# One core: the column part of each tridiagonalisation step ahead of its inner product, and the first normalisation's statistics on ScalarE

## What is computed

```python
h = maximum(layernorm(x), 0)                       # first normalisation
deg = A.sum(0) + A.sum(1) - diagonal(A);  L = diag(deg) - A
L_norm = d_inv_sqrt * L * d_inv_sqrt
_, U = eigh(L_norm)                                # 128 x 128, written out by hand in the kernel
x = x + U @ (relu((U.T @ h) @ W1 + b1) @ W2 + b2)  # first layer, for each batch
h = maximum(layernorm(x), 0)                       # second normalisation
x = x + second_layer(h)                            # two products with adj, then LSTMs over windows of 1 to 4 nodes
```

## Time and profile before

| | |
|---|---|
| median of 3 runs | 1527.23 us (1527.11 to 1527.44) |
| profiled execution | 1526.4 us, its span 1524.7 us |
| PE busy | 1196.6 us, 78% of the span |
| DVE busy | 1127.3 us, 74% |
| ACT busy | 816.7 us, 54% |
| POOL busy | 507.2 us, 33% |
| granted TensorE clock, mean | 0.938 of full |

### The profile page before, as it was taken

How to read it: one execution, slowest core, us unless ns; L and a number is a source line. 1 busy time by engine, 2 the same in 40 slices (tenths; PEclk the granted TensorE clock), 3 DMA queues, 4 the chain that set the end, 5 groups by cost and what they waited for, 6 DMA issues and landing times.

```text
span 1524.7 us, 26089 instructions
## 1 busy us (share of the span) xinstructions
PE 1196.6 (78%) x7121; PEld 1070.2 (70%) x7121; DVE 1127.3 (74%) x5950; ACT 816.7 (54%) x2699; POOL 507.2 (33%) x1426
## 2 busy tenths in 40 slices
PE   5677777777626500079999999999999999999998
PEld 4556666666515500068889899898998989989897
DVE  8999999999999999977757645555464554645545
ACT  2323222232419800012478687786877868778676
POOL 0288888888888888820000200000000000000000
PEclk9999999999959955569999999999999999999999
DMA  9300000000000000003100000000000000000001
GB/s 268 78 1 1 1 1 1 1 1 1 1 1 1 1 0 1 0 22 90 56 1 1 28 0 14 14 0 28 0 14 14 0 28 0 16 12 0 28 1 29
DMA packets 43624, 28.75 MB, mean 19 GB/s; under 512 B 1520, under 2 KB 39440, under 8 KB 43536
## 3 DMA queue, kind: packets, MB, share of 16 engines
q1 hardware_dynamic: 43536, 27.81, 6.7%
HBM read 19.42 MB, written 8.39 MB: 18 GB/s over the span
## 4 chain that ended last, share of the span: by engine, by line
PE 54%; DVE 40%; ACT 3%; issue 3%; ACTq 0%; DVEq 0%
PE bank L796 13%; PE bank L786 10%; PE bank L791 8%; PE bank L799 7%; DVE PV L1190 5%; DVE RC L1184 4%; PE bank L599 3%; DVE PV L1120 3%; DVE sc L933 2%; PE bank L716 2%; PE bank L768 2%; PE bank L760 2%; PE bank L724 2%; DVE sc L944 2%; PE bank L754 2%
## 5 line engine op out<-in xcount | busy, mean ns | idle before, releaser
L796 PE MATMUL bank<-spare,wT 128*128 128x256 f32 (+2 forms) x1408 | 311.3, 321 | 0.0
L533 ACT ACTIVATE PV<-bank,bias 128x256 f32<-128x256 f32 (+2 forms) x704 | 303.9, 435 | 0.0
L533 ACT ACTIVATE BIG<-bank,bias 128x128 f32<-128x128 f32 (+2 forms) x544 | 227.5, 418 | 121.1 <-PE bank L799 101.9
L796 PEld LDWEIGHTS bank<-spare,wT 128*128 128x128 f32 x1408 | 234.8, 191 | 13.2
L786 PE MATMUL bank<-spare,wT 128*128 128x128 f32 (+2 forms) x1088 | 228.1, 320 | 4.1 <-DVE spare L1427 2.7
L1413 DVE TENSOR_TENSOR BIG<-BIG,PV 128x128 f32<-128x128 f32 (+2 forms) x192 | 62.9, 328 | 206.1 <-ACT BIG L533 206.1
L786 PEld LDWEIGHTS bank<-spare,wT 128*128 128x128 f32 x1088 | 168.7, 190 | 22.4 <-DVE spare L1427 9.1
L799 PE MATMUL bank<-spare,wT 128*128 128x128 f32 (+2 forms) x768 | 169.7, 303 | 0.0
L425 ACT ACTIVATE sc<-bank 128x1 f32<-128x1 f32 x127 | 21.7, 171 | 257.9 <-PE bank L599 257.9
L599 PE MATMUL bank<-ident 128*128 128x2 f32 x254 | 74.4, 362 | 97.5 <-DVE ident L949 96.3
L791 PE MATMUL bank<-spare,wT 128*128 128x128 f32 (+2 forms) x768 | 141.7, 307 | 3.7 <-DVE spare L1425 1.2
(11 more groups left out here) (393 smaller groups left out, 2788.4 us busy)
## 6 DMA issues: line engine op xcount, KB each, us to landing
spare<-in_x SPq DMA_DIRECT2D x32, 256.0 KB, 4.1
out<-X SPq DMA_DIRECT2D x32, 256.0 KB, 2.4
spare<-in_L_gnn_Wih SPq DMA_DIRECT2D x4, 256.0 KB, 5.4
spare<-in_L_gnn_Whh SPq DMA_DIRECT2D x4, 256.0 KB, 5.2
W<-in_L_gnn_W SPq DMA_DIRECT2D x2, 64.0 KB, 3.2
Wg<-in_L_gnn_Wg SPq DMA_DIRECT2D x2, 64.0 KB, 2.5
adj<-in_adj SPq DMA_DIRECT2D x1, 64.0 KB, 1.7
X<-in_x SPq DMA_DIRECT2D x4, 0.5 KB, 17.0
```

The source lines that it names most:

```text
L533: last = nc.scalar.activation(gate_out[q][i][:, 0:T], gate(i, q, T), ACT.Tanh if q == GATE_G else ACT.Sigmoid, bias=bias[:, at:at + 1])
L796: last = nc.tensor.matmul(gate(i, q, T), wT[:, 0, p - 1, q * D:(q + 1) * D], xt, start=True, stop=(j == 0))
```

## The change

DVE's scalar pairs are formed in another way and order. A new pair `MU` is column 0 and 1 of `UC` times `u_t`, formed beside the reciprocal; `HV, HG` is `MU` times `h_k`. The wait for ACT's column comes ahead of `HUM, HU`, that for ACT's row ahead of `HV, HG`. `PT` (the column part) is put ahead of the inner product. `x_statistics` is taken from DVE and becomes three activations on ACT, at the end of ACT's part of a step: a copy that sums, a small one that makes minus the mean, and a square that sums. `STAT_LAG` is 2; `stat_at` puts one batch in each step from step 2 on, and two in steps 10, 20 and 30, so that all 128 are done in step 126. `variance` for the first normalisation shrinks to one operation, and `inverse` to six of the same kind written out.

```diff
-        bn_done = sem("bn_done")
+        stats_done = sem("stats_done")
...
+        MU = 8
...
-        BN_LAG = 16
+        STAT_LAG = 2
+
+        def stat_at(k):
+            return max(0, k - STAT_LAG) + sum(k > 10 * (e + 1) for e in range(BATCH - STEPS + STAT_LAG))
...
+            def x_statistics(b):
+
+                total, lower, at = ln[:, 0, b:b + 1], ln[:, 3, b:b + 1], X[:, b, :]
+                if b % (BATCH // X_CHUNKS) == 0:
+                    act.wait_ge(x_in[b // (BATCH // X_CHUNKS)], 16)
+                nc.scalar.activation(QP[0], at, ACT.Copy, accum_out=total).then_inc(stats_done, 1)
+                act.wait_ge(stats_done, 3 * b + 1)
+                nc.scalar.activation(lower, total, ACT.Copy, scale=-1.0 / D).then_inc(stats_done, 1)
+                act.wait_ge(stats_done, 3 * b + 2)
+                nc.scalar.activation(QP[1], at, ACT.Square, bias=lower,
+                                     accum_out=ln[:, 1, b:b + 1]).then_inc(stats_done, 1)
...
                 nc.scalar.activation(eB[:, k:k + 1], sign(k), ACT.Identity, scale=two_sigma(k)).then_inc(e_ready, 1)
+                for b in range(stat_at(k), stat_at(k + 1)):
+                    x_statistics(b)
...
-                if k >= BN_LAG:
-                    x_statistics(k - BN_LAG)
...
                 n_h = step(V.reciprocal(h_k, S(DEN)))
+                dve.wait_ge(hv, n_ut)
+                n_mu = step(V.tensor_scalar(S(MU, 2), UC[:, k, 0:2], u_t, None, ALU.mult))
                 dve.wait_ge(hv, n_h)
                 dve.wait_ge(u_ready, k + 1)
+                dve.wait_ge(acol_ready, k + 1)
+                n_hu = step(V.tensor_tensor(S(HUM, 2), UC[:, k, 1:3], h_k.to_broadcast([N, 2]), ALU.mult))
+                dve.wait_ge(hv, n_mu)
                 if t + 1 < N:
                     dve.wait_ge(row_ready, k + 1)
-                n_hu = step(V.tensor_tensor(S(HUM, 2), UC[:, k, 1:3], h_k.to_broadcast([N, 2]), ALU.mult))
-                n_hv = step(V.tensor_scalar(S(HV, 2), UC[:, k, 0:2], u_t, h_k, ALU.mult, ALU.mult))
+                step(V.tensor_tensor(S(HV, 2), S(MU, 2), h_k.to_broadcast([N, 2]), ALU.mult))
 
                 dve.wait_ge(pb_ready, k + 1)
-                dve.wait_ge(acol_ready, k + 1)
-                step(V.tensor_tensor_reduce(out=wB[:, live(k)], in0=banks[1][:, live(k)], in1=uk[:, live(k)],
-                                            scale=h_k, scalar=0.0, op0=ALU.mult, op1=ALU.add, accum_out=S(K3)))
                 dve.wait_ge(hv, n_hu)
                 n_pt = step(V.scalar_tensor_tensor(out=S(PT), in0=B[1][:, nxt], scalar=S(HUM), in1=S(ACOL),
                                                    op0=ALU.mult, op1=ALU.subtract))
+                step(V.tensor_tensor_reduce(out=wB[:, live(k)], in0=banks[1][:, live(k)], in1=uk[:, live(k)],
+                                            scale=h_k, scalar=0.0, op0=ALU.mult, op1=ALU.add, accum_out=S(K3)))
...
-            for b in range(STEPS - BN_LAG, BATCH):
-                x_statistics(b)
             hear(rows)
-            go(V.tensor_copy(dB[:], B[3]))
+            n_dB = go(V.tensor_copy(dB[:], B[3]))
             V.tensor_tensor(Q1, B[4], QH, ALU.mult).then_inc(q_in, 1)
-            dve.wait_ge(bn_done, BATCH)
...
-            variance(slice(0, BATCH))
+            dve.wait_ge(stats_done, 3 * BATCH)
+            V.tensor_scalar(ln[:, 1, :], ln[:, 1, :], 1.0 / D, LN_EPS, ALU.mult, ALU.add).then_inc(ln_var, 1)
             n_e = go(V.scalar_tensor_tensor(out=M[0], in0=eB[:], scalar=-1.0, in1=eB[:], op0=ALU.mult, op1=ALU.max))
+            n_E = go(V.tensor_copy(EV[:], eB[:].unsqueeze(1).to_broadcast([N, LEVELS, N])))
+            dve.wait_ge(v_, n_dB)
             n_D = go(V.tensor_copy(D4[:], dB[:].unsqueeze(1).to_broadcast([N, LEVELS, N])))
-            n_E = go(V.tensor_copy(EV[:], eB[:].unsqueeze(1).to_broadcast([N, LEVELS, N])))
...
-            inverse(slice(0, BATCH))
+            off, var, inv, shift = (ln[:, c, :] for c in range(4))
+            op(V.reciprocal(inv, inv))
+            op(V.tensor_tensor(off, inv, inv, ALU.mult))
+            op(V.tensor_tensor(off, off, var, ALU.mult))
+            op(V.tensor_scalar(off, off, -0.5, 1.5, ALU.mult, ALU.add))
+            op(V.tensor_tensor(inv, off, inv, ALU.mult))
+            V.tensor_tensor(shift, shift, inv, ALU.mult).then_inc(ln_done, 1)
```

More of the change, by code:

```diff
@@ L891, in step @@
                 return h.n
[L893 to L897, removed]
             def householder(k, before):
@@ L1377, in statistics @@
                     at = it * (STREAMS * GB) + i * GB + b
-                    V.bn_stats(stats[:, at, :], X[:, at, :]).then_inc(bn_done, 1)
+                    V.bn_stats(stats[:, at, :], X[:, at, :]).then_inc(stats_done, 1)
             for it in range(ROUNDS):
                 if it == ROUNDS - 2:
-                    dve.wait_ge(bn_done, BATCH + FIRST)
+                    dve.wait_ge(stats_done, 3 * BATCH + FIRST)
                     variance(slice(0, FIRST))
@@ L1444, in last_statistics @@
                 elif (n, i) == (CELL + 8, 3):
-                    dve.wait_ge(bn_done, 2 * BATCH)
+                    dve.wait_ge(stats_done, 4 * BATCH)
                     variance(slice(FIRST, BATCH))
```

## The result

| | before | after |
|---|---|---|
| median time | 1527.34 us (1527.11 to 1527.44, 4 runs) | 1516.64 us (1515.92 to 1516.81, 4 runs) |
| profiled execution | 1526.4 us, span 1524.7 | 1516.81 us, span 1515.1 |

The medians are 10.7 us apart, a ratio of 0.9930; the ratio on record is 0.9927, with a 95% interval of 0.9915 to 0.9939. The forecast was 1516.7.

What follows compares the result with a forecast made beforehand. The chain of waits lay on PE (54%) and DVE (40%), with POOL 9.0 us behind. DVE's 16.6 us gain, some 6 lost waiting for POOL, left 10.5: profiled 1526.4 to 1515.9, median 1516.7, range 1512.5 to 1521.

Steps and rivals of the forecast that it cites:

- main mechanism: At the sign before `eig_done`: of DVE's 16.6 us gain, 6 us turn into a wait for POOL; chance 0.74.
- (a): DVE's order inside a Householder step: 0.12 us in some 28 steps, 0.10 in 99, 13.3 us gained.
- (b): `bn_stats` taken out of DVE's step: 1.0 us gained over all, between 0 and 4.4.
- (c): DVE's seam after step 126: statistics and variance operations shrink, 4.1 us gained.
- (d): ACT's three statistics activations take 1.25 us (1.0 to 1.7) and fit the 1.84 us gap before the root.
- double steps: Steps 10, 20 and 30, two batches on ACT: 2.5 us each, over the free gap; -1.8 us in all.
- R4: Rival: Sqrt and Square not in one ACT table, two loads a step, near 1775 us; chance 0.02.
- sum on DVE's path: All DVE terms to the sign, 13.3 + 1.0 + 4.1 - 1.8 = 16.6 us gained, L1341 reached at 651.5.
- POOL's path: POOL's leaf work ends 1.3 us earlier, at 657.8, from its earlier start; 1.5 us allowed either way.
- R1: Rival: order gives under 0.04 us a step, DVE stays last at the sign; 1523.9, up to 1518 us; chance 0.10.
- R2: Rival: POOL's end follows DVE's lighter load, so the whole 16.6 us arrive; 1510.6 us; chance 0.05.
- R3: Rival: ACT's statistics ahead of the root become the bound, slower, 1562 us; chance 0.05.

Runs made afterwards that it cites:

- experiment 1: The kernel after with 15 instead of 16 of POOL's QR sweeps; 1513.66 us.
- experiment 2: The kernel before with 15 instead of 16 of POOL's QR sweeps; 1526.78 us.
- experiment 8: The kernel after without `MU`, 15 QR sweeps, plus an extra PE column product into an unread bank ahead of the real one; 1560.37 us.
- experiment 7: The kernel after without `MU` (`HV, HG` from one two-scalar instruction) and with 15 instead of 16 QR sweeps; 1510.16 us.
- experiment 5: The kernel after without `MU`: `HV, HG` again from one two-scalar instruction, the new order kept; 1517.84 us.
- experiment 4: The kernel after with the old order and no `MU` in the step, so only the statistics move to ACT; 1524.11 us.
- experiment 3: The kernel before with only the new order and `MU` in the step, `bn_stats` left on DVE; 1519.66 us.
- experiment 6: The kernel after with the square of each statistics batch on ACT done three times; 1525.82 us.

## Why the prediction was right, point by point

**The main mechanism held.** The gain on DVE's path exceeded POOL's slack, and the rest became an idle time before the sign, released by POOL's L417 (3.36 us). Experiments 1 and 2 show it from both sides.

**(a) The order: 13.3 forecast, 8.6 measured alone. This is the term that was mis-sized.** The first 16 steps gave 0.12, as forecast (R came 2.89 us after x_c and now comes 2.77), the next 16 gave 0.09. The middle ones gave 0.05 to 0.07 and the narrow ones 0.04 to 0.05, not 0.10. Two things were read wrongly. First, `PT` comes 0.13 behind `HV, HG`, not 0.08, in every part of the loop. Second, the bound "R cannot start before L606's end plus 0.03" took the product as ready too early; it is ready 0.11 us after its modelled end, as experiment 8 shows. In the earlier trace rows that is 254.79 + 0.11 = 254.90, so R at 254.98 had 0.08 us to gain and not 0.16. This second limit decides in the narrow steps: in after, R stands right at it in 23 of the last 32 steps. The bounds, 0 to 20 us, held the measured 8.6.

`MU` is the smaller half of the story. It was costed at 0.06 for `HUM, HU`, and from the reciprocal on it costs 0.07 (0.26 against 0.19). Put against the old two-scalar instruction it loses: without it DVE comes to the sign 2.8 to 2.9 us earlier (experiments 7 and 5). This was not costed as a variant of its own.

**(b) `bn_stats` out of the step: +1.0 forecast**; -1.0 by itself (experiment 4), +0.8 beside the new order (364.68 for after against 365.50 for experiment 3). The same steps agree from profile to profile within some 0.2 us (364.68 and 364.64 in after and experiment 1, 374.06 and 374.13 in before and experiment 2, 361.62 and 361.84 in experiments 5 and 7), so the two signs are repeatable. But they are not shown to be the price of `bn_stats`. Take the median step of each 16 and add up: beside the new order that gives 360.3 us with `bn_stats` (experiment 3) and 360.5 and 360.1 without (after, experiment 1), the same, and the 0.8 lies in single steps that last 0.1 to 0.3 us longer than their neighbours. Beside the old order it gives 369.2 and 369.4 with it (before, experiment 2) and 370.1 without. So in a typical step its removal gains nothing in either order. Why the single long steps fall as they do stays open.

**(c) The seam: 4.1 forecast, 3.87 measured**, and 3.88 in experiment 4.

**(d) ACT: 1.25 us forecast, 1.15 measured.** A summed output, for which there was no row, adds an instruction of 0.19 us, but that overlaps the activation and ends 0.09 us behind it (242.22 against 242.13, 242.98 against 242.89), so each adds 0.09 where up to 0.2 was taken. The double steps were put at -1.8 us and cost nothing visible: the root was only 0.05 late. The first transfer of x stalled nothing, as forecast. For the table sets the Trainium skill (ScalarE: Activation LUTs, Table sets) names no Square among the cheap functions that every set has; the measurement settles it here: Sqrt, Abs, Copy, Identity and Square alternate over 127 steps with no load in the trace, so R4 falls.

**The sum on DVE's path** was forecast at 16.6 and came to 13.45: 9.38 in the steps (374.06 - 364.68), 3.87 in the seam, 0.12 ahead of the first x_c, and the rounding of what follows.

**POOL's path: 1.3 us forecast, 1.0 measured, as the sum of two misses.** Its start gained 2.4 us (65.76 to 63.35), since the double step cost nothing and two long early steps became ordinary (the first, 3.63 to 3.06 us, and the sixth, 3.34 to 3.03); its length grew by 1.4 us, inside the 1.5 allowed. L1360 was forecast at 657.9 and stands at 658.09. So the time was near to the forecast because POOL decides it: the error in (a) moved the length of the wait (3.4 us, not 6.3), not the end. Then L1366 gained the forecast 0.3 us, and in the profiled pair the low clock took 0.64 back, which the forecast had put at nothing. That the median came within 0.1 us of the forecast is partly luck: POOL's two misses cancel to 0.3 us, and the profiled executions differ by 9.6 us and the medians by 10.7, around a forecast of 10.5. What the mechanism earned is the end of POOL as the limit, and a time inside the range.

**The rivals.** R1 would have shown no idle time before L1360; R2 would have left experiment 1 without effect. R1's condition was put too low, though: with 10.2 us to POOL's end and 3.3 from the other parts, DVE stays the last below 6.9 / 127 = 0.054 us a step, not 0.04. Measured were 8.6 / 127 = 0.068, so it was nearer than it looked. R3 was judged rightly in its mechanism: the statistics have 0.82 us to spare, and experiment 6 went through that. DVE's path grew by 11.9 us there and the time by 9.2, because the wait for POOL took the first 3.4 us. The rule that HV, HG, now an instruction with two SBUF inputs, would slow POOL (the Trainium skill, GPSIMD Engine Reference, Specifications) can't be separated here: POOL took 594.7 us with it and 593.3 without (experiment 5), less than the scatter between kernels.

## What to carry to other kernels

Before you shorten an engine's path, look for the other work that has to be there at the next common point, and subtract its slack first: here POOL's 9.0 us of slack, and the 1.0 us by which it came earlier itself, let 10.0 of DVE's 13.45 us through. (By the medians the whole change gave 10.7.) Once such a wait exists, the time no longer judges edits on the first path (`MU` cost some 3 us unseen), so take the other engine's load down in an experiment and judge them there. And take a matmul as ready by when a reader that is known to wait for it starts, not by the end in its record.

## What the hardware did that was not expected

**POOL's length for the same work varies between kernels.** POOL has 1426 instructions before and after, and the same 16 sweeps. From its first to its last leaf instruction it took 593.3 us before and in experiment 5, 593.4 in 6, 594.7 after, 596.2 in 4 and 598.1 in 3. One operation of each sweep, in three sweeps of the kernel before:

```profile
423.44 2.78 POOL L399 TENSOR_TENSOR leaf<-leaf 128x15 f32<-128x15 f32 x1
...
500.67 2.79 POOL L399 TENSOR_TENSOR leaf<-leaf 128x15 f32<-128x15 f32 x1
536.34 2.77 POOL L399 TENSOR_TENSOR leaf<-leaf 128x15 f32<-128x15 f32 x1
```

The last two are 35.7 us apart; the first two are two sweeps apart (another L399 lies between them), 38.6 us each. Beside the Householder steps, whose DVE operations are short, a sweep took 35.5 to 36.2 us in the kernel before. Behind them, with wide DVE operations, the next seven took 35.7 to 41.2 (up to 42.4 in after), and single short POOL instructions, 0.33 us at least, lasted up to 2.4. Of the 4.7 us that experiment 3 took more than before, 4.0 fall into those seven sweeps. That the differences between kernels come from where wide DVE operations fall within a sweep is likely, but no run here tries it.

**A column product in two passes is ready 0.11 us after its modelled end.** In experiment 8 R starts there in every step, 0.67 us after the product's start. In the wider steps of experiment 7, where the record is shorter, R starts as early as 0.60 us after the start, so the start is the worse mark.

**A summed output on ACT is an instruction of its own** (ACTIVATION_READ_ACCUMULATOR, 0.19 us), issued 0.20 to 0.30 us after its activation, and it overlaps that one's end: 0.09 us of it lie behind.

**The granted clock rose after 3.8 us of the same work in one kernel and after 5.1 in the other.** Experiment 2, with the program of before on PE, has 5.23 us for the same 32 matmuls where before has 5.62, and experiment 1 has 6.41 where after has 6.26. Why is open.
